# A set-up that takes the first four tiles to attention while the other four are prepared

## The reference

```python
mod = (silu(c) @ wmod).reshape(4, 6, 1, -1)      # c: 4 x 256, wmod: 256 x 1536
sa, ca, ga, sb, cb, gb = ...                     # six rows of 256 for each batch
ga, gb = sign * maximum(abs, 0.25)               # both gates clamped away from zero
h = layernorm(x) * (1 + ca) + sa
x = x + ga * attention(h)                        # own layernorm with gamma, beta; q, k, v; causal; o_proj; + h
h = layernorm(x) * (1 + cb) + sb
x = x + gb * ffn(h)                              # 704 wide, silu, top 2 of 8 low-rank experts of rank 16
```

## Time and profile before

| | |
|---|---|
| median of 3 runs | 670.26 us (670.22 to 670.79) |
| profiled execution | 669.96 us |
| its span | 668.1 us |
| PE, DVE, ACT, POOL at work | 98%, 70%, 54%, 55% of the span |
| instructions | 10913 |
| granted clock of PE, mean | 0.997 |

### The profile page before, as it was taken

One profiled execution on the slowest core, in us unless ns is written; L12 is line 12 of the kernel. 1 busy time (PEld: TensorE's weight loads), 2 busy tenths in 40 slices (PEclk: granted clock), 3 DMA queues, 4 the chain that ended last, 5 costly groups with the idle time before them and its releaser, 6 DMA issues.

```text
span 668.1 us, 10913 instructions
## 1 busy us (share of the span) xinstructions
PE 652.1 (98%) x3890; PEld 561.4 (84%) x3890; DVE 466.5 (70%) x1146; ACT 360.3 (54%) x646; POOL 369.5 (55%) x442
## 2 busy tenths in 40 slices
PE   8799999999999999999999999999999999999996
PEld 6488987888889987888889897887889998798885
DVE  5857676888785776688776677689886757547323
ACT  1766466545555547555455446564455456654543
POOL 1099366538658236657676317665666525633644
PEclk9999999999999999999999999999999999999999
DMA  8400020000000020000000001000000000000000
GB/s 308 138 1 1 2 64 0 1 1 32 0 1 32 1 65 1 0 1 33 0 1 32 1 6 59 1 1 33 1 0 27 7 1 1 1 1 1 32 0 33
DMA packets 15032, 15.47 MB, mean 23 GB/s; under 512 B 1793, under 2 KB 13697, under 8 KB 14977
## 3 DMA queue, kind: packets, MB, share of 16 engines
q1 hardware_dynamic: 14976, 14.76, 6.6%
HBM read 10.57 MB, written 4.19 MB: 22 GB/s over the span
## 4 chain that ended last, share of the span: by engine, by line
PE 84%; DVE 10%; ACT 3%; issue 1%; DMA 1%; POOL 0%; SPq 0%; DVEq 0%; ACTq 0%
PE ps L1265 78%; PE ps L1274 6%; DVE hid L1112 2%; DVE rstd L844 1%; DVE zb L864 1%; DMA xs<-in_L_attn_x 1%; DVE neg_mean L1176 1%; ACT xr L587 1%; ACT act_s L725 1%; DVE zb L867 0%; DVE stat L998 0%; DVE stat L861 0%; DVE topi L1057 0%; DVE xr L1007 0%; DVE nr_a L842 0%
## 5 line engine op out<-in xcount | busy, mean ns | idle before, releaser
L475 POOL TENSOR_TENSOR ring_lo<-hid,ring_hi 128x512 fp32r<-128x512 f32 x144 | 187.2, 1304 | 110.0 <-ACT ring_hi L733 109.4
L725 ACT ACTIVATE act_s<-ps 128x512 f32<-128x512 f32 x120 | 71.6, 597 | 123.0 <-PE ps L1265 122.4
L1112 DVE TENSOR_TENSOR hid<-act_s,ps 128x512 f32<-128x512 f32 x120 | 82.1, 684 | 78.9 <-ACT act_s L725 74.1
L733 ACT ACTIVATE ring_hi<-hid 128x512 fp32r<-128x512 f32 (+1 forms) x144 | 90.4, 627 | 5.3 <-PE ps L1265 3.5
L1265 PE MATMUL ps<-wdT_hi,ring_hi 128*128 128x256 f32 x192 | 53.2, 283 | 0.0
L1265 PE MATMUL ps<-wdT_lo,ring_hi 128*128 128x256 f32 x192 | 52.7, 280 | 0.0
L467 POOL TENSOR_TENSOR xT_lo<-tr_full,xT_hi 128x512 fp32r<-128x512 f32 x28 | 35.9, 1297 | 29.0 <-ACT xT_hi L597 29.0
L1265 PE MATMUL ps<-wdT_hi,ring_lo 128*128 128x256 f32 x160 | 44.7, 280 | 0.0
L1265 PE MATMUL ps<-vv_hi,pT_hi 128*128 128x256 f32 x144 | 42.9, 298 | 0.1
L1265 PE MATMUL ps<-tm_hi,bgT_hi 128*128 128x512 f32 x96 | 39.5, 411 | 2.4 <-DVE hid L1112 2.4
L482 POOL TENSOR_TENSOR xr<-xr,y_gb 128x256 f32<-128x256 f32 x31 | 22.6, 754 | 33.6 <-DVE y_gb L1147 33.6
(11 more groups left out here) (232 smaller groups left out, 2018.2 us busy)
## 6 DMA issues: line engine op xcount, KB each, us to landing
out<-xr SPq DMA_DIRECT2D x7, 512.0 KB, 2.9
xs<-in_L_attn_x SPq DMA_DIRECT2D x3, 1024.0 KB, 5.7
xs<-in_L_attn_x SPq DMA_DIRECT2D x2, 512.0 KB, 4.7
s_mod<-in_L_wmod SPq DMA_DIRECT2D x2, 512.0 KB, 7.6
s_qkvT<-in_L_attn_qkv SPq DMA_DIRECT2D x1, 768.0 KB, 7.4
wgT_raw<-in_L_ffn_Wg SPq DMA_DIRECT2D x1, 704.0 KB, 7.9
wuT_raw<-in_L_ffn_Wu SPq DMA_DIRECT2D x1, 640.0 KB, 8.7
wdT_raw<-in_L_ffn_Wd SPq DMA_DIRECT2D x1, 640.0 KB, 5.7
```

What stands on the lines that cost most here:

```text
L475: pool.tensor_sub(ring[1][:, place(n), :], hid[:, n % HID, :], ring[0][:, place(n), :].bitcast(fp32)).then_inc(h_lo.sem, 1)
L725: nc.scalar.activation(act_s[:, n % 2, :], ps[:, 2 * (n % 2), :], ACT.Silu).then_inc(silu_ready.sem, 1)
L733: nc.scalar.activation(ring[0][p0:P, place(n), :], hid[p0:P, n % HID, :], ACT.Copy).then_inc(h_hi.sem, 1)
L1112: V.tensor_mul(hid[:, n % HID, :], act_s[:, n % 2, :], ps[:, 2 * (n % 2) + 1, :]).then_inc(h_ready.sem, 1)
```

## The change

The order of batch 0 is written anew on all engines; batches 1 to 3 are as they were.

- **Modulation.** The scale rows of batches 1 to 3 come from one matmul each with four rows of input: `mod_row(0)` makes the four batches' rows (`scale_rows`), and `batch_rows`, made once on GpSimd, picks one row for all partitions. `s_scb` is made for batch 0 alone. The first scale copy signals by itself (`first_scale`). `gate_spread` lies in `bc` and is filled in two parts.
- **DVE.** The centres of tiles 0 to 3 stand between Newton steps; their rows, statistics and Newton steps follow with the gate clamps among them, and not the work of tiles 4 to 7. That stands behind, around the split of `xT` of the first half.
- **PE.** Transposes of tiles 0 to 3, modulation 1 to 4, queries 0 and 1, then the loop. Within the loop of batch 0: values of tiles 0 to 3 after scores 0; modulation 6 and 7 and the transposes of tiles 4 to 7 after scores 1; queries 2 and 3 after `probs_values(0)`; values of tiles 4 to 7 after `probs_values(1)`. `FIRST_PROJ` is the order of the projections, `FIRST_PROJ_BANKS` where they lie. Scores of row 4 wait for all eight. ACT and DVE follow.
- **ACT.** A small exponential at the very start. `weight_high` moves from the end of the set-up and rows 0 to 5 to rows 2 to 6.
- **GpSimd.** The value weight waits for the first shift alone, the residual rows for the second. Of `weight_low`, steps 0 to 5 stay, 6 to 8 come after the Newton steps of the second norm, and 9 to 11 (`wdT` in two parts, `adT`) behind `hid_low` 0, 2 and 4 of the feed-forward; PE waits for them where it first reads them.

The diff, cut to its core (left out: declarations, changes of index that only apply `proj_place`, `proj_bank` and `turn_bank`, and the removed lines of the set-up on DVE, ACT and PE, which stand in the listing above):

```diff
+        mod_rows = wmask[0:B, :, :].rearrange("p s n -> p (s n)")
+        scale_rows = y_gb[0:B, :, :].rearrange("p t d -> p (t d)")
+        batch_rows = bc[0:B, B - 1, SA:CA + 1, :].rearrange("p t d -> p (t d)").rearrange("p (b n) -> p b n", n=P)
+        gate_spread = bc[:, :, GA:GB + 1, :].rearrange("p b t (k n) -> p b (t k) n", n=P)
...
-        BODY_HIGH = {0: (4, 5, 6), 1: (7,), 2: (8,), 3: (9,), 4: (10,), 5: (11,)}
+        BODY_HIGH = {2: (0, 1), 3: (2, 3), 4: (4, 5, 6, 7), 5: (8, 9, 10), 6: (11,)}
...
-        MOD_JOBS = (("scale", 0), ("gate", 0), ("scale", 1), ("gate", 1), ("gate", 2), ("gate", 3), ("scale", 2), ("scale", 3))
...
+        MOD_JOBS = (("scale", 0), ("gate", 0), ("scale", 1), ("scale", 2), ("scale", 3), ("gate", 1), ("gate", 2), ("gate", 3))
...
+        FIRST_PROJ = (0, 1, 4, 5, 2, 3, 6, 7)
+        FIRST_PROJ_BANKS = (0, 1, 1, 3, 4, 5, 1, 3)
+        FIRST_TURN_BANKS = (0, 1, 1, 3)
+        W_ROUTER, W_UP = 6, 9
...
             pool.wait_ge(mod_copied, 2)
-            pool.wait_ge(first_shift, 2)
+            pool.wait_ge(first_shift, 1)
             values_weight(0)
             values_weight_low(0)
             pool.wait_ge(wvo_lo.sem, wvo_lo.at(0, 0))
+            pool.wait_ge(first_shift, 2)
             for i in range(NT):
                 pool.wait_ge(first_step, FIRST_ROWS[i])
                 residual(0, i)
-            for j in range(WEIGHT_STEPS):
+            for j in range(W_ROUTER):
                 weight_low(j)
             pool.wait_ge(mod_copied, len(MOD_JOBS))
             setup_steps = steps[1]
...
                     newton(b, LN2_A, 0, TC, it)
+                if b == 0:
+                    for j in range(W_ROUTER, W_UP):
+                        weight_low(j)
                 for k in range(KT):
                     tr_low(b, KT * NC + k, [t[:, 0, k, :] for t in xT])
...
+                        if b == 0 and ci == 0 and r in (0, 2, 4):
+                            weight_low(W_UP + r // 2)
                         if ci == 1 and r == 0:
                             out_rows(b, (2, 3))
...
+            nc.scalar.activation(lg[:, 0, :], cT[:, :, :].rearrange("p k b -> p (k b)"), ACT.Exp, scale=0.0).then_inc(unwaited, 1)
             def modulation(job):
                 what, b = MOD_JOBS[job]
...
                 act.wait_ge(product_ready, j + 1)
                 nc.scalar.activation(w[:, :, :].rearrange("p k d -> p (k d)"), ps[:, 4 + j, :], ACT.Copy,
                                      scale=scale).then_inc(product_hi, 1)
...
+            product_high(0)
+            act.wait_ge(gates_made, 1)
+            spread_gates(0, 1)
             def values_weight_high(b):
                 act.wait_ge(wvo_scaled.sem, wvo_scaled.at(b, 0))
...
             act.wait_ge(first_shift, 1)
             for i in range(TC):
                 first_normalise(i)
+            product_high(1)
+            mod_row(2)
+            attention_inputs(0, range(KT))
+            modulation(1)
             act.wait_ge(modT_ready, 1)
             nc.scalar.activation(modT[:, :, :, :].rearrange("p t k b -> p (t k b)"), ps[:, TURN_BANK, 2 * KT * B:4 * KT * B], ACT.Copy).then_inc(modT_copied, 1)
+            spread_gates(1, B)
+            values_weight_high(0)
+            queries_values(0, (0,))
+            modulation(2)
+            queries_values(0, (1,))
             modulation(3)
             modulation(4)
             modulation(5)
...
             act.wait_ge(pads_made, 3)
...
             def body(b, last):
...
+                        queries_values(b, (4, 5))
+                        act.wait_ge(first_shift, 2)
+                        for tile in range(TC, NT):
+                            first_normalise(tile)
+                    if b == 0 and i == 1:
+                        modulation(6)
+                        modulation(7)
+                        attention_inputs(b, range(KT, KT * NC))
                     if i == 1:
                         probs_high(0)
-                    if i < 2:
+                    if b == 0 and i in (2, 3):
+                        queries_values(b, ((2, 3), (6, 7))[i - 2])
+                    if b and i < 2:
                         queries_values(b, (6 + i,))
                     if b == 0:
                         for j in BODY_HIGH.get(i, ()):
...
             x_stats(first)
             dve.wait_ge(x_loaded, 16)
             x_stats(second)
             moments(range(NT))
...
+            mark(guess(0, NT))
+            settle()
+            for n, small in enumerate(first_newton(0, NT)):
+                mark(small())
+                at = steps[1]
+                if n == TC:
+                    dve.wait_ge(first_scale, 1)
+                if TC <= n < 2 * TC:
+                    ln1_centre(0, n - TC)
+                dve.wait_ge(vstep, at)
             dve.wait_ge(mod_copied, 1)
...
             settle()
             for i in first:
                 first_rows(i)
...
             for i in first:
                 first_stats(i)
             moments(first)
             mark(guess(0, TC, True))
...
+            g = gateT[:, :]
+            clamps = {3: (lambda: V.tensor_copy(g, ps[:, TURN_BANK, 0:2 * KT * B]),),
+                      4: (lambda: V.tensor_scalar(gate_sign[:, :], g, 0.0, 2.0, ALU.is_ge, ALU.mult),
+                          lambda: V.scalar_tensor_tensor(gate_size[:, :], g, -1.0, g, ALU.mult, ALU.max)),
+                      5: (lambda: V.tensor_scalar_max(gate_size[:, :], gate_size[:, :], 0.25),)}
             settle()
             for n, small in enumerate(first_newton(0, TC)):
                 mark(small())
...
+                if n == 3:
+                    dve.wait_ge(gates_turned, 1)
+                for clamp in clamps.get(n, ()):
+                    mark(clamp())
+                if n == 6:
+                    V.scalar_tensor_tensor(g, gate_sign[:, :], -1.0, gate_size[:, :], ALU.add, ALU.mult).then_inc(gates_made, 1)
+                settle()
             first_shifts(0)
             for i in second:
...
+                ln1_centre(0, i)
+            wqk_low()
+            settle()
             dve.wait_ge(loaded["ln"], 32)
             attention_scale(0, range(KT))
+            for i in second[:2]:
+                first_rows(i)
             for q in range(KT):
                 attention_low(q)
...
+            for i in second[2:]:
+                first_rows(i)
+            for i in second:
+                first_stats(i)
+            queries_values(0, (0,))
+            moments(second)
+            mark(guess(TC, TC, True))
+            queries_values(0, (1,))
+            settle()
+            for n, small in enumerate(first_newton(TC, TC)):
+                mark(small())
+                if n == 0:
+                    dve.wait_ge(modT_copied, 1)
+                    mark(V.tensor_scalar_add(modT[:, 1, :, :], modT[:, 1, :, :], 1.0))
+                settle()
+            first_shifts(TC)
             setup_steps = steps[1]
             VSTEPS = 102
...
+                    if b == 0 and i == 1:
+                        attention_scale(b, range(KT, KT * NC))
+                        for q in range(KT, KT * NC):
+                            attention_low(q)
                     if 3 <= i < 3 + TC - 1:
                         x1_stats(i - 3)
                     if i == NT:
...
                     for k in range(KT):
                         last_mm = mm(ps[:, bank, :], s_scb[:, k, b, :], s_mod[:, k, 0:2 * D], k == 0, k == KT - 1)
+                elif what == "scale":
...
                 else:
                     for t in range(2):
...
             pe.wait_ge(loaded["mod_gates"], 16 * KT)
...
+            mod_row(1)
+            def products(j, left, right):
                 for d in range(KT):
                     for k in range(KT):
                         last_mm = mm(ps[:, 4 + j, d * D:(d + 1) * D], s_qkvT[:, left, k, d * P:(d + 1) * P], right[:, k, :],
                                      k == 0, k == KT - 1)
                 last_mm.then_inc(product_ready, 1)
+            pe.wait_ge(loaded["qkv"], 16)
+            products(0, 0, s_qkvT[:, 1, :, :])
+            mod_turned(0, gates_turned)
+            pe.wait_ge(loaded["o"], 16)
+            products(1, 2, s_o)
             pe.wait_ge(loaded["mod_rest"], 16)
...
+            mod_row(2)
             def transposes(b, q, bank, k, rows):
...
+            mod_turned(1, modT_ready)
+            pe.wait_ge(consts_made, 7)
+            modulation(2)
+            modulation(3)
             pe.wait_ge(product_lo, 1)
...
+            modulation(4)
+            queries(0, (0, 1))
+            pe.wait_ge(gates_spread, 2)
+            modulation(5)
             def body(b, last):
...
                         last_mm.then_inc(scores_ready.sem, 1)
-                        if i < 2:
+                        if b and i < 2:
...
+                            values(b, range(NT // 2))
+                        if b == 0 and i == 1:
```

(55 more changed lines are left out.)

137 lines of the change are left out of this document (51 added, 86 removed).

## The result

The changed kernel takes 676.65 us, the median of 4 runs (676.19 to 678.36), against 670.24 for the kernel before in the same series: a ratio of 1.0099, 95% interval 1.0084 to 1.0114. That is slower by 6.4 us, where 6.4 was forecast over a median of 670.26. The profiled execution is the slowest of the four, 678.36, which is 1.7 over the median.

What follows compares the result with a forecast made beforehand. TensorE, at work for 98% of the span, was taken as the bound, with DVE and GpSimd taking turns. 669.96 + 2.1 (set-up) + 4.3 (feed-forward) = 676.4, plus 0.3 to the median: 676.7; range 671.6 to 679.0.

Steps and rivals of the forecast that it cites:

- The feed-forward, 4.3: Batch 0: weight_low 9 to 11 between hid_low hold DVE's chain of 128x4 instructions; hidden(6) and PE 4.3 us later.
- five or so durations over 1 us: Expected sign in the profile: on DVE, neg_mean to rstd of batch 0's feed-forward show about five such long instructions.
- The upper bound of 5.8: Feed-forward of batch 0: most that hidden(6) could be late, 106.8 + 11 x 0.2 against 103.22.
- The set-up, 2.1: Set-up of batch 0: row 4's scores start at 57.2 against 55.13, 2.1 us later, through holes of PE.
- the milestone: First product of row 4's scores on PE, at 55.13 before; the set-up's gains and losses are counted to it.
- Steps 1 and 2: Set-up, tiles 0 to 3: shift at 21.2, 3.2 us earlier; then PE ends their transposes at 24.5 (27.75 before).
- Step 4: Set-up: values_weight(0) on GpSimd collides with DVE's xT_lo; xT_lo 1 done at 29.55, not 28.3; queries start at 29.6.
- Steps 5 and 7: Set-up: DVE held by GpSimd's wvo_lo at rows 6 and 7 (1.25) and by residual rows at xT_lo 2 and 3 (1.0).
- Granted clock 1.00 throughout: Expected sign in the profile after: PE's clock never falls; a granted clock of 0.5 at the second transposes would be wrong.
- the rival that I gave 0.12: The clock falls in a new hole of PE, once or twice 1.5 us more: 678 to 679.4; chance 0.12.
- Only the set-up costs: DVE's 128x4 steps in the feed-forward get through between GpSimd's instructions, leaving +2.1: 672.4; chance 0.13.
- Only the feed-forward costs: The set-up's collisions of DVE and GpSimd miss each other, so -1.4 + 4.3: 673.2; chance 0.15.

Runs made afterwards that it cites:

- the warm profile: Changed kernel with weight_low 9 to 11 in one piece behind the second norm's two xT_lo, ahead of the router; no cold stretch in the set-up: 671.92 us.
- the thirty products: 30 unread bf16 products in PE's hole ahead of the first transposes, added to the changed kernel with all twelve weight_low before the loop (671.24 us); later also 668.94 us.
- third version of the last experiment: Changed kernel with weight_low 6 to 11 spread elsewhere, row 4's scores waiting for the seventh low copy, and 30 unread products on PE: 668.94 us.

## Why the prediction was right or wrong

**The sum** was right, 676.7 against 676.65, and that is luck in good part. In medians the feed-forward alone costs 6.1 and the set-up, with GpSimd's weights out of the way, 0.2; the forecast had 4.3 and 2.1. The feed-forward's hold has its 4.3, by a mechanism that was half right. The clock behind it, put at nothing, gives about 2, and that fills the place of a set-up term that was about 2 too large.

**The feed-forward, 4.3.** Measured 4.3, and shown by moving this part alone and by moving it away. The place, the instructions, the one that is late next (hidden(6), and PE with it) are as written. The step that failed is "each that meets a running instruction of GpSimd waits for its end". nr_h waited for four, a memset and three more, 4.53 us, until GpSimd stood still ahead of the next memset. Turns of one instruction, where GpSimd was made to keep them, cost 2.5. That the size agreed is luck of where the queue stood still: "five or so durations over 1 us" were 0.80, 4.53 and 1.38. The upper bound of 5.8 had DVE served only once GpSimd runs dry; it was not reached because four of the eleven steps were through by 106.56, two ahead of the hold and two at its end. The Trainium skill (SBUF — State Buffer, section Who interferes with whom) lets an instruction with a single input pass only outside the two-port modes, and lists `tensor_scalar`, the form of nr_h, among those that can run in one. The hold of nr_h fits that if it ran in such a mode, which no run here shows; a hold over more than one instruction of GpSimd the section does not have.

**The set-up, 2.1.** Measured 1.6 at the milestone of the profiled execution (56.75 against 55.13), and 0.2 in the median of the version that leaves this set-up as it is. Steps 1 and 2 came out (shift at 20.81, transposes to 24.3). Step 4 failed: xT_lo was not held, GpSimd was, and the queries started at 28.14, not 29.6. Steps 5 and 7 held for 1.0 and 0.5 instead of 1.25 and 1.0. The holes of PE, forecast at 1.2, 2.2, 2.7 and 1.4, were 1.84, 0.52, 1.80 and 1.50. The second is short because cold queries filled it; in the warm profile it is 1.32. On a warm clock all this is 0.2 earlier than before, 54.91, between the 53.7 without any turns and the 57.2 with all. So it was mis-sized: steps 4, 5 and 7 together held 3.5 in the forecast and 1.5 in the trace.

**The clock** made up the difference. (The 678 to 679.4 of that rival counts from 676.4; from the median it is 0.3 more.) "Granted clock 1.00 throughout" failed, and the rival that I gave 0.12 came true in part, inside the forecast's range: 1.6 of the set-up's loss is the cold chain of queries 2 and 3, and behind the 4.58 hole of the feed-forward 24 products took 7.88 instead of 5.79, 2.1 more in the profiled execution. Its sum is 669.96 + 1.6 + 4.3 + 2.1 = 677.96, with 0.4 not accounted for to 678.36. The mean clock was 0.988 in this execution and 0.993 in the other three, which were 1.3 to 2.2 faster. That they lacked the cold chain of queries 2 and 3 fits this, but they have no trace.

**The rivals.** "Only the set-up costs", 672.4, has the size of the version with all weights in front, 671.5, but that version loses its 1.2 to GpSimd's queue at row 6 and not to turns in the set-up. "Only the feed-forward costs", 673.2, was tried as that part alone and gave 676.4: it has the old set-up and so not the gain of 1.4, and the clock's share came with it. The prediction also says that the chain is dense, so what the set-up loses or gains arrives whole. That holds only while GpSimd's queue is short: in two experiments all but 0.3 of the 1.3 us won ahead of row 4 was gone again at row 6.

**Open.** Why nr_h is passed over at three borders (above). What makes the clock fall at 28 to 34 was not found either. The hole ahead of the first transposes is not needed for it, and filling it decides nothing: with the thirty products one profile was warm and the other cold. Over the ten profiles of the new set-up it goes rather with the moment at which PE's first scale products start: cold at 30 for 9.90 to 10.27 us (five), warm for 10.42 to 11.12 (four), cold again at 11.37 (one). This was not tested. What stands there in every version is the six scale products with four rows of input (2.82 us); they were not taken away alone.

## What to carry to other kernels

Deferring work of GpSimd "to where nothing waits for it" has to be checked against VectorE's smallest instructions, not its largest: a chain of 0.2 us steps on the critical path pays for every GpSimd instruction that it meets (2.5 us here), and a single step can be held over several (4.53 us here). Spread such work over places where GpSimd stands still and VectorE does nothing small, and look which queue is the bound before shortening PE's path: 1.3 us at row 4 were worth 0.3 at the second norm in one order of the weights, and in another a wait of 1.5 us that was taken out ahead of row 4 gave 1.3 at the end. And hold a forecast against its terms, not its sum: here a term too large and a term left out cancelled.

## What the runs showed of the hardware

- A VectorE instruction on 128x4 fp32 with one input, that needs 0.17 us alone, took 4.53 us (4.54 in a second kernel): it was issued while GpSimd ran a memset and held over that and the three instructions queued behind it, on 128x512 and 128x768. With GpSimd made to stand still for some 0.1 us between them it took 0.27.
- Elsewhere VectorE is let in between two GpSimd instructions that follow each other without a gap: zb at 152.57 of the kernel before took 1.15 us, and the ring_lo issued at 153.40 took 1.47 instead of 1.28.
- It goes the other way too: values_weight on GpSimd took 1.85 instead of 1.27 beside two xT_lo of VectorE, that took 0.64 each.
- The granted clock fell to 0.50 at 30 us (third version of the last experiment) while PE had been busy for ten microseconds with less than 0.1 us of waiting, and the same program (all weights in front) ran some of its executions at a mean clock of 1.00 and others at 0.99.
